# A graph layer on Trainium2: the ReLU of the radial product moves from ScalarE to VectorE, and a fifteenth group of table rows to ScalarE's queue

## The reference, cut to what matters

```python
h = relu(layernorm(x))                      # nodes
l0, l1 = h[:, :64] @ W_l1_0, h[:, 64:] @ W_l1_1      # a table row of 160 for each node
r = relu(ea @ W_fc1 / sqrt(10)) * sqrt(2)   # edges: 10 -> 100, the radial product and its ReLU
w = r @ W_fc2 / 10                          # edges: 100 -> 192, the weights
m = w * table[src] * e4                     # four kinds of message
s = segment_sum(m, dst) / 4                 # sums over each node's edges
out = x + self_interaction(h) + 0.5 * (s @ W_l2) * node_vec1 / sqrt(96)
```

## Time and profile before

| | before |
|---|---|
| median of 3 runs | 3937.83 us (3935.28 to 3940.37) |
| profiled execution | 3939.58 us |
| its span, first to last instruction | 3935.8 us |
| mean granted clock of TensorE, share of full speed | 0.863 |
| busy: TensorE / VectorE / ScalarE / GpSimd | 83% / 60% / 19% / 75% |
| gathers of GpSimd in the loop | 3031 |
| row DMAs of SyncE and ScalarE | 6656 and 7168 |

### The profile page before, as it was taken

How to read it: one execution, slowest core, us unless ns; L and a number is a source line. 1 busy time by engine, 2 the same in 40 slices (tenths; PEclk the granted TensorE clock), 3 DMA queues, 4 the chain that set the end, 5 groups by cost and what they waited for, 6 DMA issues and landing times.

```text
span 3935.8 us, 83918 instructions
## 1 busy us (share of the span) xinstructions
PE 3247.8 (83%) x17464; PEld 1918.8 (49%) x17464; DVE 2363.2 (60%) x8236; ACT 748.3 (19%) x1681; POOL 2947.5 (75%) x3119
## 2 busy tenths in 40 slices
PE   5788788888888877887888887988888888888887
PEld 4454444454444444444554444545454455555444
DVE  7455556565665656565666556556666566666655
ACT  5111112111111111111121212111112121211111
POOL 6777777777777777777777777777777777777776
PEclk8788889888998889788898889788888888989788
DMA  9565656565556565656566565656656565656655
GB/s 316 151 145 134 149 140 147 143 149 140 146 147 148 143 146 143 147 141 149 140 156 147 146 153 139 151 140 153 147 144 150 142 150 145 148 145 148 150 145 134
DMA packets 827774, 589.86 MB, mean 150 GB/s; under 512 B 535130, under 2 KB 748654, under 8 KB 826878
## 3 DMA queue, kind: packets, MB, share of 16 engines
q1 hardware_dynamic: 660752, 317.60, 31.0%
q0 software_dynamic: 149520, 255.42, 27.6%
q10 hardware_dynamic: 16990, 11.41, 1.1%
HBM read 429.06 MB, written 155.04 MB: 148 GB/s over the span
## 4 chain that ended last, share of the span: by engine, by line
PE 20%; SPq 18%; ACTq 16%; issue 15%; POOL 15%; DMA 10%; DVE 6%; ACT 2%; DVEq 0%; POOLq 0%
POOL R L867 13%; ACTq L1038 11%; SPq L930 10%; DMA R<-l_table,src 6%; PE bank L682 6%; PE bank L1199 6%; ACTq L1035 4%; PE bank L1212 3%; PE bank L1189 3%; DMA s_tiles<-E 3%; SPq L927 3%; DVE R L1116 3%; SPq L646 3%; PE bank L725 1%; DVE R L1113 1%
## 5 line engine op out<-in xcount | busy, mean ns | idle before, releaser
L867 POOL DMA_INDIRECT R<-l_table,src x3031 | 2865.7, 945 | 934.8 <-issue 843.3
L1199 PE MATMUL bank<-w,hs 100*128 100x192 f32 x6446 | 1388.0, 363 | 97.7 <-ACT hs L979 77.4
L1199 PEld LDWEIGHTS bank<-w,hs 100*128 100x128 f32 x6446 | 1181.3, 212 | 416.8 <-issue 286.0
L1113 DVE TENSOR_TENSOR R<-bank,R 128x256 f32<-128x256 f32 x1558 | 654.2, 420 | 1129.6 <-PE bank L1199 786.8
L1116 DVE TENSOR_TENSOR R<-bank,R 128x192 f32<-128x192 f32 x3116 | 954.2, 348 | 0.0
L1212 PE MATMUL bank<-R 128*32 128x320 f32 x6448 | 679.0, 495 | 307.1 <-DVE R L1116 300.3
L979 ACT ACTIVATE hs<-bank 100x512 f32<-100x512 f32 x806 | 437.4, 594 | 2159.1 <-PE bank L1189 991.3
L1100 DVE COPY E<-bank 128x320 f32<-128x320 f32 x806 | 391.8, 486 | 230.9 <-DMA s_tiles<-E 179.7
L1189 PE MATMUL bank<-ea,w1s 10*100 10x512 f32 x1612 | 515.0, 718 | 10.7 <-DMA ea<-in_ea_p 9.9
L682 PE MATMUL bank<-ZD 128*128 128x450 f32 x776 | 413.6, 688 | 100.2 <-issue 96.8
L1212 PEld LDWEIGHTS bank<-R 128*32 128x32 f32 x6448 | 143.8, 113 | 528.7 <-issue 411.7
(11 more groups left out here) (114 smaller groups left out, 898.2 us busy)
## 6 DMA issues: line engine op xcount, KB each, us to landing
s_tiles<-E SPq DMA_DIRECT2D x395, 320.0 KB
lone_act<-l_table ACTq DMA_DIRECT2D x7168, 0.6 KB
psc<-l_table SPq DMA_DIRECT2D x3584, 0.6 KB
H<-l_table SPq DMA_DIRECT2D x3072, 0.6 KB
R<-l_table,src POOLq DMA_INDIRECT x3031
ea<-in_ea_p SPq DMA_DIRECT2D x202, 224.0 KB
ZD<-s_tiles SPq DMA_DIRECT2D x97, 384.0 KB
ZD<-s_tiles SPq DMA_DIRECT2D x97, 324.0 KB
```

Of the source, the lines that this page charges most:

```text
L867: PL.indirect_dma_start(out=Y[:, g % NB, t, :], out_offset=None, in_=T, in_offset=bass.IndirectOffsetOnAxis(ap=src[:, k:k + 1], axis=0),). ...
L1113: V.tensor_tensor(p[:, :, :, 0:64], w[:, :, 0:128].rearrange("p t (s c) -> p t s c", s=2), y[:, :, 0:64].unsqueeze(2).to_broadcast([128, n ...
L1199: m = PE.matmul(b[:, o * 192:(o + 1) * 192], hs[:, g % 4, t * 128:(t + 1) * 128], w2[:, :], start=True, stop=True, skip_group_check=True)
```

## The change

The ReLU is written as one `tensor_scalar` (times `REL`, then maximum with 0) on VectorE. Groups 0 and 1 have theirs ahead of the loop; in turn g, behind the product of its last half, comes that of group g+2. ScalarE's ReLUs go. `NACT` is 15 in place of 14, and `apart` then chooses 50, 101, 154, 203, 253, 307, 356, 410, 458, 509, 560, 611, 657, 713 and 763 for ScalarE. The raw groups (41, 75, 108, 150, 183, 224, 257, 299, 332, 365, 406, 439, 480, 513, 555, 587, 620, 661, 694, 735, 767) and SyncE's (60, 121, 179, 243, 303, 361, 425, 486, 546, 607, 668, 729, 790) stay.

```diff
-NACT = 14
+NACT = 15
@@ ScalarE
-            def relu(g):
-                if g >= NG:
-                    return
-                if g >= 4:
-                    AC.wait_ge(s_wp, g - 3)
-                AC.wait_ge(s_h, g // 2 + 1)
-                AC.activation(hs[:, g % 4, :], bank[g % 2][0:100, 0:GE], ACT.Relu, scale=REL).then_inc(s_hs, 1)
...
-            for g in range(4):
-                relu(g)
             for g in range(NG):
-                if g % 2:
-                    relu(g + 3)
-                    relu(g + 4)
                 for j in at(g, 0):
                     norm(j)
@@ VectorE
+            def relu(g):
+                if g >= NG:
+                    return
+                if g >= 4:
+                    V.wait_ge(s_wp, g - 3)
+                V.wait_ge(s_h, g // 2 + 1)
+                V.tensor_scalar(hs[:, g % 4, :], bank[g % 2][0:100, 0:GE], REL, 0.0, ALU.mult, ALU.max).then_inc(s_hs, 1)
...
+            relu(0)
+            relu(1)
             for g in range(NG):
                 V.wait_ge(s_wp, g + 1)
...
                     weigh(g, u)
                     if u == 0 and g:
                         evac_sum(g - 1)
+                relu(g + 2)
                 for j in at(g, 6 + LATE):
                     residual(j, True)
```

## The result

| | before | after |
|---|---|---|
| median | 3936.56 us (3933.44 to 3940.37) | 3966.89 us (3960.35 to 3974.96) |
| ratio, 95% interval | | 1.0078 [1.0054, 1.0101] |
| profiled execution, its span | 3939.6, 3935.8 | 3960.35, 3956.2 |
| mean granted clock | 0.863 | 0.875 |

The account below looks back on a forecast made before the run. GpSimd's gathers were taken as the bound: 117 us before them, 3800 of gathers, 18.5 behind. The profiled 3939.6 less 5.0 for four gathers gave 3934.6, with the median 1.8 lower: 3933 us, range 3920 to 3958.

Parts of the forecast that it names:

- Fifteenth group of rows: GpSimd's gathers: 3027 in place of 3031, four at 1.254 us, so 5.0 us off the path.
- ScalarE's queue: ScalarE's row issues and activations: 3158 us before, 2893 after, relieved by 265 us, with rows coming no later.
- 806 ReLUs on VectorE: VectorE's turns: 0.68 us a ReLU, mostly covered by TensorE's sums; first half loses 53 to 83, regains 44 to 71 us.
- The net cost of nothing: First-half consumers: net change between -18 and +39 us, against 52.0 us of waits for gathers; GpSimd's hold stays near 10.
- VectorE busy: VectorE's busy time over the kernel: 2363 + 806 x 0.68 = 2911 us, 74%.
- The row groups move: GpSimd's ring of six: free groups at new places, three within nine turns twice; costed at 0, up to +5 us.
- D: Rival: clustered free groups hold GpSimd at the ring and cost what the fifteenth brings, +5 us, 3938; chance 0.11.
- VectorE's waits for gathers: VectorE waiting for GpSimd's gathers: the total changes by no more than some 100 us.
- Ports: Port pair VectorE shares with GpSimd: PSUM-source ReLUs would not block gathers; the contrary, 4481 us, had chance 0.02.
- The rivals: The prediction's alternative outcomes for the whole kernel; the likeliest, 3933 us with GpSimd's hold unchanged, had chance 0.47.
- C: Rival: VectorE paces the first half's consumers and the ring holds GpSimd; 31 us more, 3964; chance 0.20.
- C's sign: In the profile: GpSimd held by products for over 20 us before 1900 us.

Follow-up runs that it names:

- e2: The kernel before with 15 row groups on ScalarE in place of 14, the ReLU still on ScalarE; 3970.1 us, ratio 1.0085.
- e1: The kernel after with 14 row groups on ScalarE in place of 15, the ReLU on VectorE; 3943.4 us, ratio 1.0013.
- e4: The kernel before with an unused 682 ns instruction on VectorE each turn; 3945.8 us, ratio 1.0026.
- f8: The kernel after with a ring of seven in place of six, its 15 row groups sharing eight semaphores; 3964.1 us, ratio 1.0074.
- f7: The kernel after without ScalarE's first group, 50, so 14 groups at its other places; 3951.3 us, ratio 1.0037.

## Why the prediction was wrong

- *Fifteenth group of rows.* 3027 gathers at 1.25 us: right, 5.0 us came off the path. They vanish under 27.3 us of holds.
- *ScalarE's queue.* **This step failed**: "ScalarE is relieved by 265 us and the rows come no later", priced at nothing. It is +32.4 us by e2 and +23.5 by after against e1. Four things were wrong in it. A row was taken as 0.264 us, its instructions alone; with the gaps between them it is 0.33, and with its share of the loads 0.40, so that the shortest stretch's 512 rows take some 207 us, all of the 207 that it had. A ReLU was taken to free its whole 0.594 us, and frees 0.17: the queue isn't relieved by 265 us but occupied 68 us longer. It was asked only whether the rows arrive by their turn (they do: no product of after waits for a row of ScalarE), and not what waits behind them in the same queue: the tile copies, and TensorE behind those. And SyncE's queue was never summed. It has no busy row on the page, and it was full. Which of the two queues carries the loss is open.
- *806 ReLUs on VectorE.* 0.68 us forecast, 681 ns measured. Its waits were right: TensorE's waits for the ReLU were 44.0 + 71.1 us in the first half before. Over the whole run of after they are this, all before weight loads (us in total, times), and under the 50 us of the forecast:

```profile
  DVE hs L1088: 49.4, 91
```

- The net cost of nothing was nearly right: 5.8 us measured (e1). e4, with VectorE's length alone, is at 8.2 by the medians and 1.2 by the spans, so the two can't be told apart.
- *VectorE busy* was forecast at 2911 us and is 2791: overlapped instructions are counted once. Behind the last product it looks as worked out, with 0.33 and 0.53 us to the next start:

```profile
2004.41 0.41 DVE L1108 TENSOR_TENSOR R<-bank,R 128x256 f32<-128x256 f32 x1
2004.74 0.61 DVE L1111 TENSOR_TENSOR R<-bank,R 128x192 f32<-128x192 f32 x2
2005.27 0.68 DVE L1088 TENSOR_SCALAR hs<-bank 100x512 f32<-100x512 f32 x1
```

- *The row groups move* was priced at 0 to 5 us for clusters. Holds did come at turns 355 to 366 (11.3 us), where D had them, but behind a stretch with 10.4 of ScalarE's rows a turn; f8 rules the clusters out, and f7's missing hold at 181 to 184 speaks for the load.
- *VectorE's waits for gathers* were to move by some 100 us. They fell by 270. The ReLU alone takes 84 of it (e1), as forecast; the other 186 came with the rows, where the copies wait 94 us more for stores and TensorE 73 us more before the tile matmul.
- *Ports*: right. 945 ns a gather with 806 more PSUM reads beside them, as the Trainium skill has it for a PSUM source (VectorE: DVE Perf Modes, Why PSUM operands drop a tier): such a source keeps an instruction out of the two-port mode.
- *The rivals.* 3966.9 lies next to C's 3964, and C's sign is shown: GpSimd held over 20 us before 1900 us. Its mechanism is not: with VectorE as busy and 14 groups (e1, e4) the cost is 6 to 8 us. That its number comes near is chance. None of the rivals had the rows' load on the two queues.

## What to carry to other kernels

Sum every queue that issues DMAs as you sum an engine, gaps between its instructions and register loads included: its share stands in no busy row, and here SyncE, 98% full, stands on the page as no engine at all. Don't credit a queue with the full length of an activation that leaves it. For work spread over turns, price the densest stretch and not the mean: with 512 of ScalarE's rows in 44 turns after reached turn 50 at 380 us, as before did, but with 512 in 34 or 36 turns the rows pace the kernel. And work that is dropped into a queue costs what stands behind it there.

## What the runs showed of the hardware

- Plain DMAs of 640 bytes were issued every 0.33 us on a queue; with 32 addresses loaded in 2.3 us, 0.40 us a row. A gather of 128 such rows takes 1.25 us of GpSimd, 0.01 us a row.
- With 512 more rows other DMAs took longer. From issue to landing (pairing the trace's DMA records in order) a store of the sums took 3.80 us before, 4.05 in e2 and 4.04 after, and from a row's issue to its packet 2.02, 2.22 and 2.24 us; with the ReLU alone 3.77 and 2.05. Each row was one packet of 640 bytes. The Trainium skill (DMA: Bandwidth & Descriptors, Why a DMA increments its semaphore by 16 and not by 1) says that a transfer that uses k of the 16 DMA engines goes, from such a queue, to the lowest-numbered k. If one packet means k = 1, all rows would share one engine; the trace shows the one packet, and no run here parts that engine from the others.
- A ReLU of 100x512 fp32 out of PSUM took VectorE 681 ns and ScalarE 594 ns, and ScalarE's next DMA issue started 0.19 us after such a ReLU did, in the row shown.
